# Row maxima in a two-layer cross-attention kernel: two of three key sets folded by ScalarE's Relu and one fused VectorE instruction

## The reference, cut to what matters

```
q[h, s]   = absorbed query, 64 numbers          (computed in the "head" of a group)
k[t]      = rotated latent key, 64 numbers      t = 0 .. 1443
score     = q[h, s] . k[t]
m[h, s]   = max over t of the score             subtracted before exp
out[h, s] = sum_t exp(score - m) v[t] / sum_t exp(score - m)
```

## Time and profile before

| | us |
|---|---|
| median of 3 runs | 3318.08 |
| lowest and highest | 3308.29, 3320.56 |
| the profiled execution, its own time | 3316.05 |
| its span, first to last instruction | 3314.2 |
| mean granted clock of TensorE, share of 2.4 GHz | 0.932 |

### The profile page before, as it was taken

The page is one execution under the profiler, slowest core; times in us unless marked ns, Lnnn a source line. Parts: engine busy times, 40 slices in busy tenths (PEclk is TensorE's granted clock), DMA queues, the critical chain, the costliest instruction groups (busy, mean ns, idle before and its releaser), DMA issues. The chain is left out here.

```text
span 3314.2 us, 61706 instructions
## 1 busy us (share of the span) xinstructions
PE 2867.6 (87%) x18352; PEld 1925.3 (58%) x18352; DVE 2460.8 (74%) x4098; ACT 1485.7 (45%) x3074; POOL 1757.3 (53%) x1268
## 2 busy tenths in 40 slices
PE   5999979999798998998998999899899899896335
PEld 4777769999654555565565555556556456553123
DVE  5778754444388787887878878878788887876887
ACT  2333322222145545545545544554554554553556
POOL 0000022222267767767766666776775776764566
PEclk9889879999899999999999999999999999998566
DMA  4000010000300000000100000010010100011100
GB/s 112 0 0 0 0 48 10 10 5 10 80 11 16 21 12 21 19 16 17 24 17 16 21 19 17 16 26 7 21 26 11 22 19 16 11 48 31 47 13 24
DMA packets 130244, 71.05 MB, mean 21 GB/s; under 512 B 83582, under 2 KB 124510, under 8 KB 129880
## 3 DMA queue, kind: packets, MB, share of 16 engines
q1 hardware_dynamic: 129944, 67.45, 8.2%
HBM read 56.95 MB, written 10.04 MB: 20 GB/s over the span
## 5 line engine op out<-in xcount | busy, mean ns | idle before, releaser
L1195 POOL TENSOR_TENSOR c_psum<-c_p 120x800 f32<-120x800 f32 (+1 forms) x384 | 768.0, 2003 | 454.9 <-ACT c_p L1483 232.2
L1483 ACT ACTIVATE c_p<-c_s_ps 120x400 f32<-120x400 f32 (+1 forms) x1536 | 657.3, 507 | 475.6 <-PE c_s_ps L1644 458.0
L1279 DVE TENSOR_REDUCE c_mpart<-c_m_ps 128x1 f32<-128x484 f32 x1080 | 655.3, 650 | 159.6 <-PE c_m_ps L1551 158.1
L1656 PE MATMUL c_o_ps<-c_p,c_val 120*64 120x400 f32 (+1 forms) x3072 | 621.5, 528 | 0.0
L1306 DVE TENSOR_TENSOR c_acc<-c_acc,c_psum 120x800 f32<-120x800 f32 x256 | 398.2, 1555 | 53.0 <-POOL c_psum L1195 50.5
L1551 PE MATMUL c_m_ps<-c_kmax,c_q 64*128 64x484 f32 x1080 | 313.6, 463 | 114.9 <-DVE c_mpart L1279 93.8
L1186 POOL TENSOR_TENSOR l_rr<-c_psum,l_rr 96x400 f32<-96x400 f32 x256 | 260.6, 1039 | 193.5 <-DVE l_rr L1328 193.3
L1551 PEld LDWEIGHTS c_m_ps<-c_kmax,c_q 64*128 64x128 f32 x1080 | 139.2, 189 | 344.2 <-DVE c_mpart L1279 247.4
L1656 PEld LDWEIGHTS c_o_ps<-c_p,c_val 120*64 120x64 f32 (+1 forms) x3072 | 190.5, 138 | 251.5 <-issue 163.7
L1587 PE MATMUL c_s_ps<-c_xt,l_a 128*96 128x400 f32 x1536 | 310.3, 352 | 10.7 <-DVE l_rr L1328 8.2
L1640 PE MATMUL c_s_ps<-c_q,c_k 64*120 64x400 f32 (+1 forms) x1536 | 302.0, 366 | 2.3 <-ACT c_p L1483 2.3
(11 more groups left out here) (256 smaller groups left out, 4990.7 us busy)
## 6 DMA issues: line engine op xcount, KB each, us to landing
c_rdb<-l_denominators SPq DMA_DIRECT2D x128, 100.0 KB, 2.7
c_kv<-in_ctx SPq DMA_DIRECT2D x32, 360.0 KB
c_mrow<-c_mneg SPq DMA_DIRECT2D x288, 0.5 KB, 2.0
x_rows<-in_x SPq DMA_DIRECT2D x4, 800.0 KB
x_spill<-x_rows SPq DMA_DIRECT2D x8, 400.0 KB
l_xa<-x_spill SPq DMA_DIRECT2D x8, 400.0 KB
c_xr<-x_spill SPq DMA_DIRECT2D x32, 100.0 KB
x_spill<-c_xr SPq DMA_DIRECT2D x32, 100.0 KB
```

The costliest lines, as they stand in the source:

```text
L1195: g.tensor_tensor(psum[0:k, u % 2, :], p[0:k, 2 * u % 4, :], p[0:k, (2 * u + 1) % 4, :], ALU.add).then_inc(psum_ready, 1)
L1279: v.tensor_reduce(mpart[:, t, bank:bank + 1], m_ps[:, bank, 0:4 * KP], AX.X, ALU.max, negate=True).then_inc(mpart_ready, 1)
L1483: a.activation(p[0:k, w % 4, i * HALFQ:(i + 1) * HALFQ], s_ps[0:k, (2 * w + i) % 4, 0:HALFQ], ACT.Exp).then_inc(exp_ready, 1)
L1656: mm = pe.matmul(o_ps[i * DL:(i + 1) * DL, 0:HALFQ], val[0:k, j % 2, r, :], p[0:k, w % 4, i * HALFQ:(i + 1) * HALFQ], start=(r == 0), stop ...
```

## The change

The second and third key sets are no longer compared by two reductions. With k0, k1, k2 the three sets, the kernel now computes max(q.k1, q.k2) = q.k1 + max(0, q.(k2 - k1)):

- `round_keys` writes k2 - k1 (bank 2 of the turned keys less the second part of kd) into slot 1 of both halves of kmax, and k0 stays in the lower half of slot 0, k1 in the upper half (ScalarE). ScalarE makes one copy fewer, VectorE one write more.
- A tile's three units are now "rise" (difference keys), "low" (k0) and "mid" (k1). For two tiles the order is rise, rise, low, mid, low, mid; for a single tile rise, low, mid. Banks are taken in turn (unit number modulo 3).
- ScalarE writes the Relu of the rise bank to SBUF (`rise_unit`, `rise_tile`; the buffers are tiles that are free at that time: xt in the groups, parts of k1 and k2 in the head). In a group it stands after the exponentials of its pair.
- VectorE reduces the low bank as before. For the mid bank it issues one `tensor_tensor_reduce`: (bank + Relu) x -1, minimum along the row, started from the low bank's result, with the sum written over the Relu, and the minimum straight into `mneg`. The combining reductions are gone.
- A unit's matmul waits for whoever released unit n - 3: ScalarE (rise), VectorE's reduction (low) or the fused instruction (mid). In the head a tile waits for all three.
- GpSimd's first `difference` also waits for the difference keys. SP's row loads keep their order and wait for the tile counts of `mneg_ready`.

UNIT_SLOTS, all jobs, the scores, the values and the sums are as they were. The core of the diff:

```diff
         def tile_units(tiles):
             for t in tiles[::2]:
-                yield from ((t, 0, 0), (t, 1, 1), (t, 2, 0))
                 if t + 1 in tiles:
-                    yield from ((t + 1, 1, 1), (t + 1, 0, 0), (t + 1, 2, 1))
+                    yield from ((t, "rise", 0), (t + 1, "rise", 1), (t, "low", 0), (t, "mid", 1), (t + 1, "low", 0), (t + 1, "mid", 1))
+                else:
+                    yield from ((t, "rise", 1), (t, "low", 0), (t, "mid", 1))
...
+        def next_in(bank, n):
+            return n + (bank - n) % 3
+
+        def released(n):
+            t, kind, half = UNITS[(n - 3) % NMU]
+            return {"rise": rise_ready, "low": mpart_ready, "mid": mneg_ready}[kind], (n - 3) // NMU * NMT + t + 1
...
                 def difference(b, r):
                     if r == NT - 2:
                         g.wait_ge(kf_ready, PRIMED + (b + 1) * 3)
+                        g.wait_ge(kmax_low, PRIMED + (b + 1) * 3)
...
                 def round_keys(b):
                     v.wait_ge(kf_ready, PRIMED + b * 3 + 1)
                     v.tensor_copy(klow[:, 0, :], m_ps[0:DL, 0, 0:4 * KP]).then_inc(kmax_low, 1)
-                    v.wait_ge(kmax_high, PRIMED + b * 2 + 2)
-                    v.tensor_copy(klow[:, 1, :], m_ps[0:DL, 2, 0:4 * KP]).then_inc(kmax_low, 1)
+                    v.wait_ge(kf_ready, PRIMED + b * 3 + 3)
+                    for dst in (klow, khigh):
+                        v.tensor_tensor(dst[:, 1, :], m_ps[0:DL, 2, 0:4 * KP], kd[:, 4 * KP:8 * KP], ALU.subtract).then_inc(kmax_low, 1)
...
+                def reduce_low(it, j, t, bank):
+                    v.tensor_reduce(mpart[:, t:t + 1], m_ps[:, bank, 0:4 * KP], AX.X, ALU.max, negate=True).then_inc(mpart_ready, 1)
+
+                def reduce_mid(it, j, t, bank, rise):
+                    v.wait_ge(rise_ready, PRIMED + it * TG + j * NMT + t + 1)
+                    v.wait_ge(mpart_ready, PRIMED + it * TG + j * NMT + t + 1)
+                    v.sem_inc(m.carrier, 1)
+                    v.tensor_tensor_reduce(rise, m_ps[:, bank, 0:4 * KP], rise.bitcast(F32), -1.0, mpart[:, t:t + 1],
+                                           ALU.add, ALU.min, mneg[:, t:t + 1]).then_inc(mneg_ready, 1)
+
                 def reduce_tile(gi, t):
                     v.wait_ge(maxs_ready, PRIMED + gi * NMG + 3 * t + 3)
-                    v.tensor_reduce(mneg[:, t:t + 1], m_ps[:, :, 0:4 * KP], AX.XY, ALU.max, negate=True).then_inc(mpart_ready, 3)
+                    reduce_low(gi, 0, t, 1)
+                    reduce_mid(gi, 0, t, 2, head_rises[t % 2])
...
-                    v.tensor_reduce(mpart[:, t, bank:bank + 1], m_ps[:, bank, 0:4 * KP], AX.X, ALU.max, negate=True).then_inc(mpart_ready, 1)
-                    if n % NMU in COMBINED:
-                        tiles = slice(*COMBINED[n % NMU])
-                        v.wait_ge(mpart_ready, PRIMED + it * NMG + n + 1)
-                        v.tensor_reduce(mneg[:, tiles], mpart[:, tiles, :], AX.X, ALU.min).then_inc(mneg_ready, 1)
+                    if kind == "low":
+                        reduce_low(it, j, t, n % 3)
+                    if kind == "mid":
+                        reduce_mid(it, j, t, n % 3, rises[(j * NMT + t) % 2])
...
                         a.activation(kd[:, k * 4 * KP:(k + 1) * 4 * KP], m_ps[0:DL, k, 0:4 * KP], ACT.Copy).then_inc(kf_ready, 1)
-                        if k > 0:
-                            a.activation(khigh[:, k - 1, :], m_ps[0:DL, k, 0:4 * KP], ACT.Copy).then_inc(kmax_high, 1)
+                    a.activation(khigh[:, 0, :], m_ps[0:DL, 1, 0:4 * KP], ACT.Copy).then_inc(kmax_high, 1)
...
+                def rise_unit(it, n):
+                    j, k = divmod(n, NMU)
+                    t, kind, half = UNITS[k]
+                    a.wait_ge(maxs_ready, PRIMED + it * NMG + n + 1)
+                    a.wait_ge(mneg_ready, PRIMED + it * TG + j * NMT + t - 1)
+                    a.activation(rises[(j * NMT + t) % 2], m_ps[:, n % 3, 0:4 * KP], ACT.Relu).then_inc(rise_ready, 1)
...
                                 if what == "keys":
                                     copy_keys(it * G + at)
+                            for n in units_at(j, u % BP * 2 + half):
+                                if UNITS[n % NMU][1] == "rise":
+                                    rise_unit(it, n)
...
-                    pe.wait_ge(mpart_ready, PRIMED + it * NMG + last_in(bank, n) + 1)
-                    pe.matmul(m_ps[:, bank, 0:4 * KP], q1[rows, j, q], kmax[rows, bank // 2 if half == 0 else bank - 1, :],
+                    free_bank(it, n)
+                    pe.matmul(m_ps[:, n % 3, 0:4 * KP], q1[rows, j, q], kmax[rows, 1 if kind == "rise" else 0, :],
                               start=True, stop=True).then_inc(maxs_ready, 1)
...
```

More of the change, by code:

```diff
@@ L845, in phase_l1_attention @@
     NMG = G * NMU
[L846 to L848 removed]
+    TG = G * NMT
+    ROW_TILES = ((0, 2), (2, 4), (4, 6), (6, 7), (7, 9), (9, 11), (11, 13))
     NU = G * CH * NT
@@ L886, in phase_l1_attention @@
         warm = sb("c_warm", [1, 1])
+        head_rises = [x[:, 0:4 * KP] for x in (k1[1], k2[1])]
+        rises = [x[:].rearrange("p k t -> p (k t)")[:, 0:4 * KP] for x in xt]
         s_ps = ps("c_s_ps", [128, 4, 512])
@@ L901, in phase_l1_attention @@
         maxs_ready, mpart_ready, mneg_ready = count("c_maxs_ready"), count("c_mpart_ready"), count("c_mneg_ready")
+        rise_ready = count("c_rise_ready")
         row_loaded = [sem(f"c_row_loaded{i}") for i in range(CH)]
@@ L955, in phase_l1_attention @@
         assert all(units_at(j, KEYS[j]).start == NMU * (j + 1) for j in KEYS)
[L957 to L964, removed]
+        def next_in(bank, n):
[3 more added lines that the diff above has]
+            return {"rise": rise_ready, "low": mpart_ready, "mid": mneg_ready}[kind], (n - 3) // NMU * NMT + t + 1
+        AFTER_DEN = {next_in(0, units_at(j, s).start): (j, s // 15) for j in range(G) for s in (3, 15) if (j, s) not in ((0, 3), (G - 1, 15))}
+        AFTER_PROJECT = {next_in(2, units_at(j, 15).start): j for j in range(1, G - 1)}
         HEAD_STEPS = {10: (0, 1), 11: (2,), 12: (3,), 13: (4, 5), 15: (6, 7, 8)}
@@ L1020, in load_combined @@
                 def load_combined(it, j, n):
-                    sp.wait_ge(mneg_ready, PRIMED + it * GCB + j * NCB - 3 + n)
+                    sp.wait_ge(mneg_ready, PRIMED + it * TG + j * NMT + ROW_TILES[n][1])
                     sp.sem_inc(m.carrier, 1)
-                    for t in range(*list(COMBINED.values())[n]):
+                    for t in range(*ROW_TILES[n]):
                         load_tile(t)
@@ L1466, in head @@
                             copy_keys(gi * G)
+                        if what == "max":
+                            rise_tile(gi, at[2])
                         for n in HEAD_STEPS.get(i, ()):
@@ L1524, in maxima_tile, with free_bank @@
                 def maxima_tile(gi, t):
-                    pe.wait_ge(mpart_ready, PRIMED + gi * NMG + 3 * t)
+                    pe.wait_ge(rise_ready, PRIMED + gi * TG + t)
+                    pe.wait_ge(mpart_ready, PRIMED + gi * TG + t)
+                    pe.wait_ge(mneg_ready, PRIMED + gi * TG + t)
                     low, high, q = slice(0, DL), slice(DL, 128), slice(starts[t], starts[t] + 128)
-                    pe.matmul(m_ps[:, 0, 0:4 * KP], q1[low, 0, q], klow[:, 0, :], start=True, stop=True)
-                    pe.matmul(m_ps[:, 1, 0:4 * KP], q1[high, 0, q], khigh[:, 0, :], start=True, stop=True)
-                    mm = pe.matmul(m_ps[:, 2, 0:4 * KP], q1[low, 0, q], klow[:, 1, :], start=True, stop=True)
+                    pe.matmul(m_ps[:, 0, 0:4 * KP], q1[high, 0, q], khigh[:, 1, :], start=True, stop=True)
+                    pe.matmul(m_ps[:, 1, 0:4 * KP], q1[low, 0, q], klow[:, 0, :], start=True, stop=True)
+                    mm = pe.matmul(m_ps[:, 2, 0:4 * KP], q1[high, 0, q], khigh[:, 0, :], start=True, stop=True)
                     mm.then_inc(maxs_ready, 3)
+                def free_bank(it, n):
+                    done, count = released(n)
+                    pe.wait_ge(done, PRIMED + it * TG + count)
                 def maxima_unit(it, n):
                     j, k = divmod(n, NMU)
-                    t, bank, half = UNITS[k]
+                    t, kind, half = UNITS[k]
                     rows, q = slice(half * DL, (half + 1) * DL), slice(starts[t], starts[t] + 128)
@@ L1663, in job @@
                             if what == "absorb":
-                                pe.wait_ge(mpart_ready, PRIMED + it * NMG + issued)
+                                free_bank(it, next_in(2, issued))
                                 pe.wait_ge(x_added, PRIMED + it * G)
@@ L1667, in job @@
                             if what == "den":
-                                pe.wait_ge(mpart_ready, PRIMED + it * NMG + last_in(0, issued) + 1)
+                                free_bank(it, next_in(0, issued))
```

(6 more changed lines are left out.)

26 lines of the change are left out of this document (16 added, 10 removed).

## The result

Six runs of each kernel gave a median of 3331.68 us after the change (3328.17 to 3338.71) and 3318.25 us before (3308.29 to 3326.33). The ratio is 1.0045, with a 95% interval of 1.0025 to 1.0064: the changed kernel is slower by some 13 us, small but outside the noise. The forecast was 3238. The profiled execution took 3333.63 us, and its span is 3331.1.

A forecast was written before the change was run, and what follows sets the result against it. VectorE's late reductions were taken to hold up TensorE; per-group waits fall from 23.6 to 14.6 us, 72 us over eight groups, plus 8 in the heads. 3316.05 - 80 = 3236 profiled, predicted 3238 us, range 3140 to 3360.

The forecast's parts named there:

- Special jobs fill the rest: TensorE's group timeline: beyond 19 late pairs totalling 23.6 us, special jobs (keys, projection, denominators) were set aside.
- At nothing: Items priced at zero, such as the hidden third write of rounded keys; 21 us if its cover goes.
- Waits of maxima for the Relu, 8.3 us a group: TensorE's mid matmuls wait for ScalarE's late Relu in 15 rise pairs: 8.3 us per group.
- VectorE's remainder, 6.3: Seven places per group where slot b's first reduction stays late behind the addition, 0.9 us each: 6.3 us.
- The ceiling of 24 us per group: TensorE's waits for late VectorE in 19 pairs, 23.6 us: at most about 24 us per group, 192 us in all.
- Rival 1: All VectorE waits vanish because ScalarE reaches the Relu in time: 200 us gained, 3118 us; chance 0.13.
- The head, 8 us: In the head, seven 1656 ns reductions become 1.42 us; 1 us net gained per head, 8 us over eight.
- Rival 3: ScalarE's queue delays the Relu, TensorE waiting 1.5 us in each of 22 rise pairs: 3430 us; chance 0.12 with milder forms.
- Rival 4: Nothing measurable: half of the ScalarE queue's price offsets the gain, 3300 to 3335 us; chance 0.13.
- Rivals 2 and 5: Slow fused instruction at 1.5 us, 3450 us, chance 0.06; Relu reloading ScalarE's tables, 3600 us and more, chance 0.03.
- groups near 204 us: Sign of being right: a group's length falls to near 204 us, from the 213.3 us window before.
- the last of the "wrong" signs: Sign of being wrong: groups stay at 213 us, with VectorE's idle time grown by all it saved.

The follow-up runs named there:

- e5: Changed kernel with slot a's Relus right after the pair's exponentials, ahead of drain and rounding steps, and keys' transposes waiting bank by bank: 3268.4 us, ratio 0.986.
- e1: Kernel before the change with its unit reductions in the groups cut from 484 to 310 columns, nothing moved to ScalarE: 3263.19 us, ratio 0.9848.
- e9: Changed kernel with the groups' Relus at their unchanged place but only 8 of 484 columns wide: 3317.02 us, ratio 0.9988 to the kernel before.
- e3: Changed kernel with slot a's Relus right after the pair's four exponentials, before drain and both key tiles' rounding steps: 3273.53 us, ratio 0.9874 to before.

## Why the prediction was wrong

**Step that failed: "Special jobs fill the rest".** The forecast set aside the pairs with keys and denominators and gave them no new price; not even its list "At nothing" has them. But these jobs take m_ps banks in the same rotation, so the change altered who gives each bank up and when. They lost 8.2 us per group, 66 us in all (311.2 to 377.0). With the Relu moved and the keys' wait split (e5) the job pairs are at 313.4 and the time is 50 us under before. The check that would have found it: for every user of a bank, not only the one in the diff, ask who releases it now and what stands ahead of the releaser on its engine. The waits for a bank before the denominators and before turn_keys were in the code.

**Terms of the sum.**
- Fused instruction at 0.80 us: measured 0.805. Relu 0.56: 0.577. VectorE's busy time per group 22 us less: 21.5. Right.
- Waits of maxima for the Relu, 8.3 us a group: (43.1 + 19.6)/8 = 7.8 by TensorE's rows, but only 43.1/8 = 5.4 of it at maxima; the rest is at the denominators. The size was right partly by luck.
- VectorE's remainder, 6.3: 39.3/8 = 4.9 by the rows. About right.
- Net 9.0 us per group in the pairs dealt with: 57.7/8 = 7.2. Over-sized, by 14 us in all.
- The ceiling of 24 us per group, "to be had": no run came near it. Rival 1 rested on it, and so did the 23.6 as a start of the sum. e1 took 28% off each reduction, left the rest alone, and got 53 us of 192; the most that any kernel gained in the other pairs is 67 us (e9). In pair 22, for one, TensorE waits 1.94 us for VectorE in before and 1.92 in e1: an addition of 2.35 and of 3.17 us stands ahead of the reduction there.
- The head, 8 us: next to nothing. The seven stretches between groups lost 1.5 us together.

Put together: forecast -80; head +8, other pairs +14, jobs +66, which is +8, and the stage shows +7.6. The jobs are thus 66 of the 88 us that the forecast was off by.

**The rivals.** Rival 3, ScalarE's queue, named the right mechanism: GpSimd's delays and rounding steps in front of the Relu; e3 against e9 shows it. It looked for the price at the mid matmuls, where the row stayed low (43.1/8 = 5.4 us a group, where it asked for over 18). The price was at the denominators and the keys. Rival 4, nothing measurable, held the number, within 3301 to 3335, at a chance of 0.13; the measured interval says slower, by a little less than the 0.5% bound. Rivals 2 and 5 fell: no slow fused instruction, and the table loads stayed at x7. Rival 1, 3118, was never near; the best kernel took 3253.63.

**The range** held the time, for it reached across to rival 4; that is luck and not the mechanism. The signs to look for, as written, all came out "right", groups near 204 us among them. But that one is empty: in the window above the group takes 203.8, and the same cut before is 203.2, not 213.3. The window of 213.3 us in the earlier trace rows began 1.4 us earlier and reached 8.7 us into the head. What did happen is in substance the last of the "wrong" signs: the group did not get shorter, though VectorE was busy 21.5 us less. A length by which a forecast is to be judged needs two named events as its ends.

## What to carry to other kernels

When a buffer in a rotation changes hands, list every user of the rotation and, for each, the engine that frees it and what that engine's queue holds ahead. Short work that others wait for belongs ahead of work that itself waits for a third engine; here that order was worth 58 us where two thirds of the duration were worth 15. A wait for several buffers at once, cheap while VectorE's reductions freed them all (11.7 us of waits), cost 40.3 when different instructions freed them, and splitting it was worth 37.

## What the runs showed of the hardware

- The fused tensor-tensor with a running minimum leaves two records, 722 ns and a read-out of 83 ns. "VectorE: DVE Perf Modes" of the Trainium skill (Two Vector instructions with no wait between them) says so of operations that also write out their accumulator; the trace agrees.
- The fused instruction reads a bank of PSUM and a tile of SBUF, the addition to acc two tiles of SBUF. Both run at times when GpSimd adds; the fused instruction at 1580.14, for one, lies wholly inside the addition of GpSimd that is shown third. Their rows after (ns min/median/max, first and last start):

```profile
L1285 DVE CUSTOM_DVE_ANT_0 c_xt<-c_m_ps,c_xt,c_mpart x360: 720/722/725, 983.5 to 3021.1; 128x484 fp32r<-128x484 f32 x180
L1324 DVE TENSOR_TENSOR c_acc<-c_acc,c_psum x256: 978/1020/3729, 992.2 to 3051.0; 120x800 f32<-120x800 f32 x128
...
1579.57 1.87 POOL L1200 TENSOR_TENSOR c_psum<-c_p 120x800 f32<-120x800 f32 x1 [1.03 <-DVE c_acc L1324]
```

  The one spreads over 5 ns, the other from 0.98 to 3.73 us. "SBUF — State Buffer" of the Trainium skill (Who interferes with whom) says that two SBUF inputs contend with a GpSimd instruction that reads SBUF and that at most one, outside the two-port modes, does not; the trace agrees. So the forecast's 0.80 held and its 1.5 did not come.
- The Relu, between exponentials and copies, brought no table load: ScalarE's line of loads in the stage stands at x7 after, as in the earlier trace rows.
- The clock fell shortly after a rest. TensorE's busy times and clock over the rest of pair 15, over the transposes behind it and over the values behind those (columns as for the windows above):

```profile
1576.00:1581.00 5.00, 1.70 (x16) 1.20 (x14) 4.16 (x6) 1.80 (x5) 3.97 (x3) 1.00 0.02 2
1581.20:1582.50 1.30, 1.28 (x12) 1.17 (x12) 0.07 (x1) 0.67 (x2) 1.01 (x2) 1.00 0.06 0
1582.50:1586.50 4.00, 4.00 (x18) 1.85 (x18) 3.64 (x5) 1.39 (x3) 0.00 (x0) 0.57 0.34 88
```

  Five microseconds with 1.70 busy at a clock of 1.00, 1.3 us of transposes still at 1.00, and then 0.57, near the 1.2 GHz level, for four microseconds in which TensorE was busy throughout. The values took 2.91 us in place of 1.56. By that the wait of 3.5 us cost at least 1.3 us more than its length. Behind the wait of 2.48 us in pair 7 the values, at 1545.89, took 2.83 us.
